# New step orders in three stages of a four-layer kernel, and the soft-MoE normalising products moved from GpSimd to VectorE

## The chip, the cores and the metric

One NeuronCore of a Trainium2 chip runs the whole program. The metric is device microseconds for one launch, lower is better. The kernel before takes 1416.57 us (median of three runs, 1414.6 to 1417.07). The profiled execution took 1420.51 us, of which 1418.7 us lie between its first and last instruction.

## The reference, cut to what matters

The input x is 8 batches of 256 tokens by 128 channels. Four layers follow, each added to x:

```python
x = x + L0_ffn(L0_cond(x))   # per-batch LoRA; gated 8-head attention; gated 8-expert GELU MoE
x = x + L1_ffn(L1_cond(x))   # one SiLU expert per batch; top-k routed GELU experts; layernorm
x = x + L2_ffn(L2_cond(x))   # two of eight tanh-GELU skills + a shared one; soft MoE:
#   logits = x @ phi.T + phi_b, as 64 experts x 32 slots
#   D = softmax(logits over slots); C = softmax(logits over experts)
#   X~ = sum over all tokens of all batches D * x;  Y~ = tanh(layernorm(X~)) @ expert_w
#   Y = sum over experts and slots C * Y~
x = x + L3_ffn(L3_cond(x))   # masked per-batch weights; 16-head rope attention; rmsnorm;
                             # SwiGLU shared + top-2 of 8 experts; rmsnorm
```

L1's routing denominator sums over batches, and so does X~. That cuts the program into stages with a full stop between them.

## The kernel before, in words

All activations stay on chip. The stages are A (L0 and the dense expert of L1), B (the routed experts of L1, the skills of L2, D and X~), a short middle part (Y~), and D (C, Y, and all of L3). Between A and B the routing of all batches is worked out on VectorE and masks pass through a DMA.

In each stage every engine runs its own in-order list of steps, written out as text: `ORDER_A`, `ORDER_B` and `ORDER_D` (L109, L149, L196), with one string for each of SP, PE, ACT, DVE and POOL. A word such as `SI0.3` is step SI0 of batch 3. `walk` (L636) splits the string and calls the stage's step function on each word, so the text alone sets the order of instructions on an engine. Semaphore waits inside the steps hold the data dependences, and nothing else ties the engines together. An engine whose next step is not ready stands still, whatever is ready behind it. Several batches are in flight at once, and the lists differ only in how they interleave.

PSUM is 8 banks, nearly all single-buffered. In stage A four banks (`wide`) hold first the spread router weights (PE SPR0, read by ACT RW0 and RW1), then the hidden units of the MoE (PE MH0, MH1, read by ACT GU0, GU1 with Gelu), then the second spread weights (PE SPR1, read by DVE S8M0, S8M1). One bank (`tail`) serves VT, MOE, UG0, UG1, DN and L1G in turn.

The steps of one batch in stage A, in dependence order: COND, LN0, NH0, NT0, AF0, LOG0, the gate chain (GA0, GB0, GX0, GE0, GTR0), SPR0, RW, S8A, QK (PE L805), QKC, SC, MXA, EX (the attention's Exp), PT, PTC, VT (PE L815), AT, S8B, O1 (PE L839), LN1 to SPR1 (the second gate chain, with GX1), MH, GU, S8M, MOE (PE L862), X1, UG0, SI0 (Silu, L1308), HM0 (DVE L1638), UG1, SI1, HM1, DN (PE L879), L1G, LA, LX (Exp), L1.

In stage B a batch has HID, BC, Z, LN, ZN, ZT (L1's routed experts; HID is a Gelu on ACT), six pairs SG0 to SG5 and SU0 to SU5 (the skills; SG is a tanh-Gelu), UC (PE L965), UT (PE L971), and four rounds of LG, MT, SH, with XT and MC (the soft MoE; SH is an Exp on ACT, L1365, and on DVE the sums and products of D, L1770 to L1774). PE's LG of a round waits until ACT's Exp of the round before has read the bank (L987 after L1365).

In stage D, CL0 to CL7 make exp(logits) in `eC` [128, 16, 256] (PE L1067, ACT L1391), CSA and CSB (POOL) and CSUM (DVE, PE) add it up, REC (DVE L1841) takes the reciprocal `rC`, and CN0 to CN3 multiply a quarter of `eC` each by it, a 128 x 1024 product. CN0 and CN1 are on DVE (L1846), CN2 and CN3 on POOL (L2056). Y0 to Y3 (PE L1080) each use one quarter. The rest is L3: S, V, Q, K, RQ, RK, QM, MX0 to MX3, NM, TS0 to TS3 (attention), AV, AVT, SA, SAT, WO, X5T, G3, FF0, FF1 (Silu), SO, RT0, RT1 with RM0, RM1 (DVE L1936), RR, FIN, OUT.

ScalarE works from a loaded function table. Exp, Gelu, tanh-Gelu and Silu stand in different tables here, and the compiler puts an `ACT_TABLE_LOAD` in front of a step whose function is not in the table at hand. Copy, Identity, Square and Tanh need none. The order of ACT's steps so sets how many loads there are.

Of the kernel before, what the change touches and what calls it, by code (L numbers as in the profile page):

```python
# [66 lines left out]
def _constants():  # L67
# [51 lines left out]
    MH0.4 LOG0.6 UG1.3 MH1.4 DN.3 PT.5 GTR1.4 L1G.3 SPR1.4 GTR0.6 VT.5 COND.7 SPR0.6 AT.5 MOE.4 O1.5 QK.6 NT1.5
    UG0.4 SC.6 NT0.7 LOG1.5 MH0.5 LOG0.7 UG1.4 MH1.5 DN.4 PT.6 GTR1.5 L1G.4 SPR1.5 GTR0.7 VT.6 SPR0.7 AT.6 MOE.5  # L120
    O1.6 QK.7 NT1.6 UG0.5 SC.7 LOG1.6 MH0.6 UG1.5 MH1.6 DN.5 PT.7 GTR1.6 L1G.5 SPR1.6 VT.7 AT.7 MOE.6 O1.7 UG0.6
    UG1.6 NT1.7 DN.6 LOG1.7 MH0.7 L1G.6 MH1.7 GTR1.7 SPR1.7 MOE.7 UG0.7 UG1.7 DN.7 L1G.7""",
    "ACT": """
# [14 lines left out]
    GB1.3 GA0.5 GE1.3 HM1.2 GB0.5 GE0.5 LA.2 S8M0.3 L1.2 S8M1.3 S8B0.4 S8A0.5 S8B1.4 S8A1.5 X1.3 LN0.6 LN1.4
    NH0.6 NH1.4 MXA.5 HM0.3 GA1.4 GB1.4 GA0.6 GE1.4 HM1.3 GB0.6 GE0.6 LA.3 S8M0.4 L1.3 S8M1.4 S8B0.5 S8A0.6
    S8B1.5 S8A1.6 X1.4 LN0.7 LN1.5 NH0.7 NH1.5 MXA.6 HM0.4 GA1.5 GB1.5 GA0.7 GE1.5 HM1.4 GB0.7 GE0.7 LA.4 S8M0.5  # L140
    L1.4 S8M1.5 S8B0.6 S8A0.7 S8B1.6 S8A1.7 X1.5 LN1.6 NH1.6 MXA.7 HM0.5 GA1.6 GB1.6 HM1.5 GE1.6 LA.5 S8M0.6
    L1.5 S8M1.6 S8B0.7 S8B1.7 X1.6 LN1.7 HM0.6 NH1.7 HM1.6 GA1.7 GB1.7 LA.6 GE1.7 L1.6 S8M0.7 S8M1.7 X1.7 HM0.7
# [10 lines left out]
    HID0.0 BC0.0 HID1.0 BC1.0 Z.0 ZT.0 HID0.1 BC0.1 SG0.0 HID1.1 SU0.0 SG1.0 BC1.1 SU1.0 SG2.0 Z.1 SU2.0 SG3.0  # L153
    SU3.0 SG4.0 ZT.1 SU4.0 SG5.0 SU5.0 UC.0 LG0.0 SG0.1 UT.0 HID0.2 SG1.1 SU0.1 MT0.0 HID1.2 SH0.0 SU1.1 SG2.1
    BC0.2 LG1.0 SU2.1 SG3.1 SG4.1 MT1.0 SU3.1 SH1.0 SG5.1 SU4.1 LG2.0 BC1.2 XT0.0 MT2.0 SU5.1 SH2.0 XT1.0 LG3.0
    UC.1 MT3.0 Z.2 SH3.0 MC.0 UT.1 LG0.1 XT2.0 MT0.1 XT3.0 SH0.1 ZT.2 HID0.3 LG1.1 HID1.3 BC0.3 MT1.1 SG0.2
    SH1.1 SU0.2 SG1.2 LG2.1 SU1.2 SG2.2 XT0.1 SG3.2 MT2.1 BC1.3 SU2.2 SG4.2 SH2.1 SU3.2 SG5.2 LG3.1 SU4.2 XT1.1
    Z.3 MT3.1 SU5.2 SH3.1 MC.1 UC.2 XT2.1 LG0.2 XT3.1 ZT.3 UT.2 HID0.4 BC0.4 MT0.2 SG0.3 SH0.2 SU0.3 SG1.3 LG1.2
    SU1.3 SG2.3 HID1.4 BC1.4 SG3.3 MT1.2 SU2.3 SH1.2 SG4.3 SU3.3 LG2.2 SG5.3 XT0.2 Z.4 MT2.2 SU4.3 SH2.2 XT1.2
    LG3.2 SU5.3 ZT.4 MT3.2 UC.3 SH3.2 MC.2 SG0.4 UT.3 LG0.3 SU0.4 XT2.2 SG1.4 HID0.5 MT0.3 XT3.2 SH0.3 SU1.4  # L160
    SG2.4 LG1.3 SU2.4 SG3.4 HID1.5 BC0.5 SG4.4 MT1.3 SU3.4 SH1.3 SG5.4 SU4.4 LG2.3 BC1.5 XT0.3 MT2.3 SU5.4 SH2.3
    XT1.3 LG3.3 UC.4 MT3.3 Z.5 SH3.3 MC.3 UT.4 LG0.4 XT2.3 MT0.4 XT3.3 SH0.4 ZT.5 HID0.6 LG1.4 HID1.6 BC0.6
    MT1.4 SG0.5 SH1.4 SU0.5 SG1.5 LG2.4 SU1.5 SG2.5 XT0.4 SG3.5 MT2.4 BC1.6 SU2.5 SG4.5 SH2.4 SU3.5 SG5.5 LG3.4
    SU4.5 XT1.4 Z.6 MT3.4 SU5.5 SH3.4 MC.4 UC.5 XT2.4 LG0.5 XT3.4 ZT.6 UT.5 HID0.7 BC0.7 MT0.5 SG0.6 SH0.5 SU0.6
    SG1.6 LG1.5 SU1.6 SG2.6 HID1.7 BC1.7 SG3.6 MT1.5 SU2.6 SH1.5 SG4.6 SU3.6 LG2.5 SG5.6 XT0.5 Z.7 MT2.5 SU4.6
    SH2.5 XT1.5 LG3.5 SU5.6 ZT.7 MT3.5 UC.6 SH3.5 MC.5 SG0.7 UT.6 LG0.6 SU0.7 XT2.5 SG1.7 MT0.6 XT3.5 SH0.6
    SU1.7 SG2.7 LG1.6 SU2.7 SG3.7 SG4.7 MT1.6 SU3.7 SH1.6 SG5.7 SU4.7 LG2.6 XT0.6 MT2.6 SU5.7 SH2.6 XT1.6 LG3.6
# [6 lines left out]
    ZT.3 UT.2 HID0.4 MT0.2 SG0.3 SH0.2 SG1.3 SG2.3 HID1.4 SG3.3 MT1.2 SH1.2 SG4.3 SG5.3 MT2.2 SH2.2 ZT.4 MT3.2
    UC.3 SH3.2 MC.2 SG0.4 UT.3 SG1.4 HID0.5 MT0.3 SH0.3 SG2.4 SG3.4 HID1.5 SG4.4 MT1.3 SH1.3 SG5.4 MT2.3 SH2.3
    UC.4 MT3.3 SH3.3 MC.3 UT.4 MT0.4 SH0.4 ZT.5 HID0.6 HID1.6 MT1.4 SG0.5 SH1.4 SG1.5 SG2.5 SG3.5 MT2.4 SG4.5
    SH2.4 SG5.5 MT3.4 SH3.4 MC.4 UC.5 ZT.6 UT.5 HID0.7 MT0.5 SG0.6 SH0.5 SG1.6 SG2.6 HID1.7 SG3.6 MT1.5 SH1.5
    SG4.6 SG5.6 MT2.5 SH2.5 ZT.7 MT3.5 UC.6 SH3.5 MC.5 SG0.7 UT.6 SG1.7 MT0.6 SH0.6 SG2.7 SG3.7 SG4.7 MT1.6
# [1967 lines left out]
```

## Time and profile before

| what | us |
|---|---|
| median of three runs | 1416.57 |
| profiled execution | 1420.51 |
| its span | 1418.7 |
| PE matmul busy | 1128.4 (80%) |
| DVE busy | 764.0 (54%) |
| ACT busy | 497.6 (35%) |
| POOL busy | 213.2 (15%) |
| stage A, COND.0 to the last step | 24 to 380 |
| stage B | 442 to 877 |
| stage D | 900 to 1418.7 |

Busy time is the union of an engine's instructions. PE is the matmul queue and PEld the weight loads beside it. "Idle before" in brackets is the time in which an engine stood still, with the instruction that released it. PEclk is the granted TensorE clock, 1.0 being full speed.

### The profile page before, as it was taken

The numbers are of one execution on the slowest core, as the hardware profiler recorded it, in microseconds if no ns is written. First come the engines' busy times: TensorE is split into PE (matmuls) and PEld (weight loads), VectorE is DVE, ScalarE is ACT, GpSimd is POOL, SyncE is SP. The second block draws the span as 40 slices with busy tenths as digits, with TensorE's granted clock in tenths as the row PEclk, the third lists the DMA queues.
The fourth block names the chain that finished last, engine by engine and source line by source line (L and its number), as shares of the span: only waits on it lengthen the run. The fifth ranks groups of instructions, "written<-read, shape, count | busy, mean of one in ns | idle before, by whom it ended". The sixth has DMA issues, their size and how long they took to land.

```text
span 1418.7 us, 17725 instructions
## 1 busy us (share of the span) xinstructions
PE 1128.4 (80%) x6726; PEld 802.2 (57%) x6726; DVE 764.0 (54%) x1667; ACT 497.6 (35%) x740; POOL 213.2 (15%) x176
## 2 busy tenths in 40 slices
...
DMA packets 13035, 34.96 MB, mean 25 GB/s; under 512 B 3680, under 2 KB 7440, under 8 KB 12179
## 3 DMA queue, kind: packets, MB, share of 16 engines
...
q0 software_dynamic: 32, 0.01, 0.0%
...
## 4 chain that ended last, share of the span: by engine, by line
PE 39%; issue 32%; DVE 12%; ACT 7%; POOLq 4%; DVEq 2%; POOL 1%; ACTq 0%; DMA 0%
PE ps L1080 4%; PE ps L805 4%; PE ps L1213 3%; PE ps L1067 3%; PE ps L815 3%; PE ps L1140 2%; PE ps L862 2%; PE ps L839 2%; PE ps L1156 2%; PE ps L1013 1%; PE ps L1120 1%; DVE arena L1865 1%; POOLq L2025 1%; ACT L1264 1%; ACT L1281 1%
## 5 line engine op out<-in xcount | busy, mean ns | idle before, releaser
L1418 ACT ACTIVATE arena<-ps 128x2048 f32<-128x2048 f32 x32 | 60.1, 1879 | 106.4 <-PE ps L1144 106.4
L1865 DVE TENSOR_REDUCE arena<-ps 128x8 f32<-128x2048 f32 x32 | 73.2, 2287 | 28.1 <-PE ps L1120 28.1
L1013 PE MATMUL ps<-arena 128*128 128x128 f32 x512 | 74.4, 306 | 12.5 <-DVE xacc L1783 6.5
L987 PE MATMUL ps<-arena,uR 128*128 128x512 f32 x128 | 73.7, 659 | 12.6 <-ACT arena L1365 12.2
L1013 PEld LDWEIGHTS ps<-arena 128*128 128x128 f32 x512 | 69.7, 217 | 19.9 <-issue 11.4
L1067 PE MATMUL ps<-uR,arena 128*128 128x256 f32 x256 | 74.0, 387 | 1.4 <-DVE arena L1820 1.4
L1080 PE MATMUL ps<-arena 128*128 128x256 f32 x256 | 64.6, 403 | 10.7 <-DVE arena L1846 10.7
L1213 PE MATMUL ps<-arena 128*128 128x512 f32 x128 | 66.2, 665 | 3.1 <-DVE xacc L1936 2.0
L1391 ACT ACTIVATE arena<-ps 128x512 f32<-128x512 f32 x64 | 38.3, 599 | 78.1 <-PE ps L1068 78.1
L1080 PEld LDWEIGHTS ps<-arena 128*128 128x128 f32 x256 | 50.0, 201 | 26.5 <-DVE arena L1846 12.7
L1770 DVE TENSOR_REDUCE arena<-arena 128x32 f32<-128x1024 f32 x32 | 39.0, 1219 | 48.0 <-ACT arena L1365 48.0
L958 PE MATMUL ps<-x2R,arena 128*128 128x256 f32 x192 | 54.6, 408 | 4.5 <-DVE arena L1751 4.5
L805 PE MATMUL ps<-arena 128*128 128x256 f32 x256 | 58.1, 385 | 0.0
L950 PE MATMUL ps<-x2R,arena 128*128 128x256 f32 x192 | 53.2, 401 | 5.4 <-DVE x2R L1743 3.1
L2056 POOL TENSOR_TENSOR arena<-arena,y1C 128x1024 f32<-128x1024 f32 x16 | 43.1, 2713 | 93.4 <-DVE y1C L1841 93.4
L805 PEld LDWEIGHTS ps<-arena 128*128 128x128 f32 x256 | 48.8, 193 | 7.0
L1140 PE MATMUL ps<-arena,x1C 32*128 32x256 f32 x512 | 44.3, 433 | 9.8 <-ACT arena L1418 7.3
L1760 DVE TENSOR_REDUCE arena<-ps 128x32 f32<-128x1024 f32 x32 | 39.2, 1225 | 22.9 <-PE ps L988 20.8
L965 PE MATMUL ps<-arena 128*128 128x256 f32 x192 | 47.1, 404 | 4.1 <-DVE arena L1751 3.9
L1346 ACT ACTIVATE arena<-ps 128x512 f32<-128x512 f32 x48 | 28.7, 598 | 59.2 <-PE ps L950 59.0
L1067 PEld LDWEIGHTS ps<-uR,arena 128*128 128x128 f32 x256 | 38.8, 190 | 18.8 <-issue 4.0
L1774 DVE TENSOR_TENSOR arena<-arena 128x1024 f32<-128x1024 f32 x32 | 47.2, 1474 | 2.4
...
## 6 DMA issues: line engine op xcount, KB each, us to landing
...
```

The lines of the kernel that those rows point to most:

```text
L805: last = mm(mid[:, j * T:(j + 1) * T], w0[w][:, e, :], S8a[u][:, e, :], start=e == 0, stop=e == E - 1)
L950: last = mm(low[:, 2, j * T:(j + 1) * T], w[:, 2 * h + j, :], x2R[:, b, :], start=True, stop=True)
L958: last = mm(low[:, 3, j * T:(j + 1) * T], w[:, 4 + 2 * h + j, :], x2R[:, b, :], start=True, stop=True)
L987: mm(o, uR[:, b, k * P:(k + 1) * P], phiC[:, col:col + 512], start=True, stop=False)
L1013: last = mm(high[:, 2, t * P:(t + 1) * P], eD[h][:, k, col:col + P], uT[u][:, k, :], start=k == 0, stop=k == 1)
L1067: mm(o, phiC[:, st_ * P:(st_ + 1) * P], uR[:, b, :], start=True, stop=False)
L1080: last = mm(low[:, 1, 0:T], ytl[:, t, :], eC[u][:, t, :], start=t == 0, stop=t == ST - 1)
L1140: mm(scores[:, c, h * T:(h + 1) * T], kR[u][row, t * P:(t + 1) * P], qm[u][row, g, :], start=True, stop=False)
L1213: last = mm(low[:, 2 + c, :], pm[:, 2 + j, k * P:(k + 1) * P], w2e[:, j, c * 512:(c + 1) * 512], start=j == 0, stop=j == 1)
L1418: av(pexp[:, t, gp].rearrange("p c h t -> p (c h t)"), scores[:, :, :].rearrange("p c t -> p (c t)"), ACT.Exp, scale=SCALE3).then_inc(s.sc ...
L1774: V.tensor_tensor(ev, ev, dsum.unsqueeze(2).to_broadcast([P, 32, PSLOT]), ALU.mult).then_inc(s.D_ready, 1)
L1865: V.tensor_reduce(nm[:, k, :, 2 * gp:2 * gp + 2], scores[:, :, :].rearrange("p c (h t) -> p c h t", h=2), X, ALU.max, negate=True).then_in ...
```

## The change

The change has two parts. The first rewrites the order texts of stages A, B and D. Each list holds the same words as before except CN2 and CN3. The interleaving of batches is another one. Lines of stage A's ACT and PE lists around batches 2 to 4, and of the middle and end of stage B:

```diff
 ORDER_A, ACT
-    GU1.1 DN.0 GTR1.1 GX0.3 PTC.2 GTR0.3 LX.0 VC.2 RW0.3 RW1.3 QKC.3 AF1.2 SI0.1 AF0.4 EX.3 GU0.2 GX1.2 SI1.1
-    GU1.2 DN.1 GTR1.2 GX0.4 PTC.3 GTR0.4 LX.1 VC.3 RW0.4 RW1.4 QKC.4 AF1.3 SI0.2 AF0.5 EX.4 GU0.3 GX1.3 SI1.2
+    GX0.4 VC.3 PTC.3 GX1.2 GU0.2 GU1.2 GTR0.4 GTR1.2 AF1.3 RW0.4 SI0.2 RW1.4 AF0.5 SI1.2 GX1.3 GU0.3 DN.2 GX0.5
+    QKC.4 GTR1.3 LX.2 GU1.3 EX.4 VC.4 PTC.4 GTR0.5 RW0.5 SI0.3 RW1.5 SI1.3 QKC.5 DN.3 AF1.4 AF0.6 LX.3 EX.5
+    GX1.4 VC.5 PTC.5 GU0.4 GU1.4 GTR1.4 GX0.6 GTR0.6 AF1.5 SI0.4 RW0.6 RW1.6 SI1.4 GU0.5 GX1.5 GU1.5 QKC.6 DN.4
 ORDER_A, PE
-    SPR1.2 GTR0.4 VT.3 COND.5 SPR0.4 AT.3 MOE.2 O1.3 QK.4 NT1.3 UG0.2 SC.4 NT0.5 LOG1.3 MH0.3 LOG0.5 UG1.2 MH1.3
-    DN.2 PT.4 GTR1.3 L1G.2 SPR1.3 GTR0.5 VT.4 COND.6 SPR0.5 AT.4 MOE.3 O1.4 QK.5 NT1.4 UG0.3 SC.5 NT0.6 LOG1.4
+    L1G.2 GTR1.3 MH1.3 SC.4 VT.4 SPR1.3 PT.4 GTR0.5 AT.4 COND.6 MOE.3 SPR0.5 UG0.3 O1.4 UG1.3 QK.5 DN.3 NT1.4
+    SC.5 L1G.3 NT0.6 LOG1.4 VT.5 PT.5 MH0.4 AT.5 MH1.4 LOG0.6 GTR1.4 SPR1.4 O1.5 MOE.4 GTR0.6 NT1.5 UG0.4 COND.7
+    SPR0.6 LOG1.5 UG1.4 MH0.5 MH1.5 QK.6 DN.4 GTR1.5 SC.6 L1G.4 SPR1.5 NT0.7 VT.6 PT.6 LOG0.7 MOE.5 AT.6 GTR0.7
 ORDER_B, PE
-    UC.3 SH3.2 MC.2 SG0.4 UT.3 LG0.3 SU0.4 XT2.2 SG1.4 HID0.5 MT0.3 XT3.2 SH0.3 SU1.4
-    LG3.7 MT3.7 SH3.7 MC.7 XT2.7 XT3.7""",
+    SG0.5 HID0.6 LG2.3 SU0.5 XT0.3 HID1.6 MT2.3 SG1.5 XT1.3 SH2.3 SU1.5 SG2.5 BC0.6 SU2.5 LG3.3 SG3.5 BC1.6
+    SG4.5 MT3.3 SG5.5 SH3.3 Z.6 SU3.5 LG0.4 XT2.3 SU4.5 MC.3 MT0.4 SU5.5 SH0.4 XT3.3 LG1.4 UC.5 MT1.4 ZT.6 UT.5
+    SH3.5 SU3.7 MC.5 SU4.7 LG0.6 XT2.5 MT0.6 SU5.7 SH0.6 XT3.5 LG1.6 UC.7 MT1.6 UT.7 SH1.6 LG2.6 XT0.6 MT2.6
```

Just before UC.7 the old PE list of stage B has `SH2.6 XT1.6 LG3.6`, the new one `SH0.6 XT3.5 LG1.6`. In stage D the new lists are nearly the old ones. Each batch's TS1 to TS3, RT1 and Y0 to Y3 are interleaved differently on PE, FIN comes ahead of X3 on DVE, and FF1.0 comes next to FF0.0 on ACT, no longer after TS0.1.

The second part moves CN2 and CN3:

```diff
 ORDER_D, DVE  (and the like for every batch; CN2, CN3 leave the POOL list)
-    CSUM.0 REC.0 CN0.0 CN1.0 X3.0 RQ.0
+    CSUM.0 REC.0 CN0.0 CN1.0 CN2.0 CN3.0 X3.0 RQ.0
 step_d, PE
-                    if q < 2:
-                        pe.wait_ge(s.C_ready, at(b, 3, 1 + q))
-                    else:
-                        pe.wait_ge(s.Cp_ready, at(b, 2, q - 2))
+                    pe.wait_ge(s.C_ready, at(b, 4, q))
 step_d, DVE
-                    if b > 0:
-                        dve.wait_ge(s.Cp_ready, at(b - 1, 2, 1))
-                    V.reciprocal(rC, low[:, 0, 0:T]).then_inc(s.C_ready, 1)
-                if n in ("CN0", "CN1"):
+                    V.reciprocal(rC, low[:, 0, 0:T])
+                if n in ("CN0", "CN1", "CN2", "CN3"):
-                    dr()
+                    if q == 0:
+                        dr()
 step_d, POOL
-                if n in ("CN2", "CN3"):
-                    pool.wait_ge(s.C_ready, at(b, 3, 0))
-                    G.tensor_tensor(some, some, rC..., ALU.mult).then_inc(s.Cp_ready, 1)
```

## Rows read from the trace of the kernel before

**Rows 1.** Windows by stage (stretch, its us): PE, PEld, DVE, ACT, POOL busy, clock, DMA share, GB/s.

```profile
22.00:380.00 358.00, 294.44 (x1752) 254.33 (x1752) 158.51 (x650) 152.26 (x235) 25.85 (x48) 0.91 0.05 18
442.00:877.00 435.00, 375.80 (x1672) 244.75 (x1671) 268.38 (x392) 165.69 (x229) 39.57 (x29) 0.94 0.06 22
925.00:1418.70 493.70, 416.07 (x3050) 273.30 (x3048) 264.52 (x410) 161.02 (x250) 97.25 (x68) 0.91 0.01 3
```

**Rows 2.** Windows in stage A: two whole batch periods, and two short stretches.

```profile
173.68:215.74 42.06, 35.52 (x221) 31.42 (x220) 19.46 (x80) 19.84 (x30) 3.23 (x6) 0.92 0.04 10
215.74:258.99 43.25, 37.91 (x222) 33.18 (x221) 19.52 (x80) 19.80 (x30) 3.23 (x6) 0.84 0.04 10
196.00:204.00 8.00, 3.17 (x14) 2.44 (x14) 2.88 (x22) 7.88 (x12) 0.69 (x1) 0.98 0.00 1
204.00:216.00 12.00, 10.29 (x66) 9.23 (x65) 5.87 (x31) 4.62 (x10) 0.00 (x0) 0.73 0.12 34
```

**Rows 3.** Timeline of PE in stage A: VT.1, QK.2, VT.5, O1.7.

```profile
73.04 3.74 PE L815 MATMUL ps<-arena 128*128 128x128 f32 x32
100.84 7.10 PE L805 MATMUL ps<-arena 128*128 128x256 f32 x32
252.63 6.51 PE L815 MATMUL ps<-arena 128*128 128x128 f32 x32 [0.21 <-DVE arena L1649]
344.68 3.74 PE L839 MATMUL ps<-arena 128*128 128x128 f32 x32
```

**Rows 4.** Chain of waits in stage A, 192 to 206 us: start, us, what.

```profile
192.27 1.28 ACT L1308
...
201.20 1.28 ACT L1308
...
203.54 1.96 PE ps L879 x4
```

**Rows 5.** Table loads by line, first and last of eleven groups: xcount | busy, mean ns.

```profile
L1346 ACT ACT_TABLE_LOAD x26 | 33.4, 1283 | 0.5
...
L1232 ACT ACT_TABLE_LOAD x1 | 1.3, 1283 | 1.6 <-PEq L2140 1.6
```

**Rows 6.** Stage B: timeline of PE at UT.1 and UT.7.

```profile
515.70 0.39 PE L971 MATMUL ps<-cst,uR 128*128 128x128 f32 x2
...
823.14 0.44 PE L971 MATMUL ps<-cst,uR 128*128 128x128 f32 x2 [0.42 <-ACT uR L1350]
```

**Rows 7.** Window of three batch periods of stage B.

```profile
569.51:726.44 156.93, 139.64 (x642) 91.92 (x642) 102.40 (x151) 67.07 (x91) 16.25 (x12) 0.97 0.09 31
```

**Rows 8.** Chain of waits in stage B's last part: the Exp of three rounds.

```profile
842.51 1.03 ACT arena L1365
...
855.81 1.03 ACT arena L1365
...
863.97 1.03 ACT arena L1365
```

**Rows 9.** The products by source line: ns min/median/max, first and last start.

```profile
L1846 DVE TENSOR_TENSOR arena<-arena,y1C x16: 1227/3137/3405, 917.4 to 1304.8; 128x1024 f32<-128x1024 f32 x16
L2056 POOL TENSOR_TENSOR arena<-arena,y1C x16: 2337/2350/3328, 917.4 to 1303.6; 128x1024 f32<-128x1024 f32 x16
L1774 DVE TENSOR_TENSOR arena<-arena x32: 1225/1226/3017, 483.7 to 866.7; 128x1024 f32<-128x1024 f32 x32
```

**Rows 10.** Stage D: Y.0 on PE, CN.5 on DVE, the loads of FF1.0 and TS1.1.

```profile
920.87 8.75 PE L1080 MATMUL ps<-arena 128*128 128x256 f32 x32 [5.35 <-DVE arena L1846]
1188.76 6.42 DVE L1846 TENSOR_TENSOR arena<-arena,y1C 128x1024 f32<-128x1024 f32 x2
1011.52 1.28 ACT L1442 ACT_TABLE_LOAD   x1
1013.43 1.28 ACT L1418 ACT_TABLE_LOAD   x1
```

**Rows 11.** Window of one batch period of stage D.

```profile
1180.39:1236.31 55.92, 50.59 (x388) 33.83 (x388) 35.59 (x53) 20.41 (x32) 13.66 (x9) 0.97 0.01 3
```

More of the change, by code:

```diff
@@ L118 @@
-    DN.2 PT.4 GTR1.3 L1G.2 SPR1.3 GTR0.5 VT.4 COND.6 SPR0.5 AT.4 MOE.3 O1.4 QK.5 NT1.4 UG0.3 SC.5 NT0.6 LOG1.4
[L119 to L122, printed above, removed]
@@ L129 @@
-    GU1.4 DN.3 GTR1.4 GX0.6 PTC.5 GTR0.6 LX.3 VC.5 RW0.6 RW1.6 QKC.6 AF1.5 SI0.4 AF0.7 EX.6 GU0.5 GX1.5 SI1.4
-    GU1.5 DN.4 GTR1.5 GX0.7 PTC.6 GTR0.7 LX.4 VC.6 RW0.7 RW1.7 QKC.7 AF1.6 SI0.5 EX.7 GU0.6 SI1.5 GX1.6 GU1.6
-    DN.5 GTR1.6 PTC.7 LX.5 VC.7 SI0.6 SI1.6 AF1.7 DN.6 GU0.7 GX1.7 LX.6 GU1.7 GTR1.7 SI0.7 SI1.7 DN.7 LX.7""",
+    QK.1 NT1.0 NT0.2 VT.1 SC.1 LOG1.0 MH0.0 PT.1 MH1.0 LOG0.2 AT.1 GTR1.0 SPR1.0 O1.1 MOE.0 GTR0.2 NT1.1 UG0.0
+    COND.3 SPR0.2 LOG1.1 UG1.0 MH0.1 MH1.1 QK.2 DN.0 GTR1.1 SC.2 L1G.0 SPR1.1 NT0.3 VT.2 PT.2 LOG0.3 MOE.1 AT.2
@@ new lines @@
+    GTR0.3 UG0.1 COND.4 SPR0.3 O1.2 UG1.1 NT0.4 QK.3 DN.1 NT1.2 SC.3 L1G.1 LOG0.4 LOG1.2 VT.3 PT.3 MH0.2 AT.3
+    MH1.2 GTR1.2 GTR0.4 COND.5 SPR1.2 O1.3 MOE.2 NT1.3 SPR0.4 UG0.2 LOG1.3 NT0.5 UG1.2 MH0.3 LOG0.5 DN.2 QK.4
+    L1G.2 GTR1.3 MH1.3 SC.4 VT.4 SPR1.3 PT.4 GTR0.5 AT.4 COND.6 MOE.3 SPR0.5 UG0.3 O1.4 UG1.3 QK.5 DN.3 NT1.4
+    SC.5 L1G.3 NT0.6 LOG1.4 VT.5 PT.5 MH0.4 AT.5 MH1.4 LOG0.6 GTR1.4 SPR1.4 O1.5 MOE.4 GTR0.6 NT1.5 UG0.4 COND.7
+    SPR0.6 LOG1.5 UG1.4 MH0.5 MH1.5 QK.6 DN.4 GTR1.5 SC.6 L1G.4 SPR1.5 NT0.7 VT.6 PT.6 LOG0.7 MOE.5 AT.6 GTR0.7
@@ new lines @@
+    UG0.5 SPR0.7 O1.6 UG1.5 QK.7 DN.5 NT1.6 SC.7 L1G.5 LOG1.6 VT.7 PT.7 MH0.6 AT.7 MH1.6 GTR1.6 SPR1.6 O1.7
+    MOE.6 NT1.7 UG0.6 LOG1.7 MH0.7 UG1.6 MH1.7 GTR1.7 SPR1.7 DN.6 L1G.6 MOE.7 UG0.7 UG1.7 DN.7 L1G.7""",
+    "ACT": """
+    AF0.0 GX0.0 GTR0.0 RW0.0 RW1.0 AF0.1 QKC.0 EX.0 GX0.1 VC.0 PTC.0 GTR0.1 RW0.1 RW1.1 QKC.1 AF1.0 AF0.2 VC.1
+    EX.1 GU0.0 PTC.1 GX1.0 GU1.0 GTR1.0 GX0.2 GTR0.2 AF1.1 SI0.0 RW0.2 RW1.2 SI1.0 GU0.1 GX1.1 GU1.1 QKC.2 DN.0
+    GTR1.1 EX.2 LX.0 AF0.3 VC.2 PTC.2 GX0.3 GTR0.3 SI0.1 RW0.3 RW1.3 SI1.1 AF0.4 QKC.3 DN.1 AF1.2 EX.3 LX.1
@@ new lines @@
+    GX0.4 VC.3 PTC.3 GX1.2 GU0.2 GU1.2 GTR0.4 GTR1.2 AF1.3 RW0.4 SI0.2 RW1.4 AF0.5 SI1.2 GX1.3 GU0.3 DN.2 GX0.5
+    QKC.4 GTR1.3 LX.2 GU1.3 EX.4 VC.4 PTC.4 GTR0.5 RW0.5 SI0.3 RW1.5 SI1.3 QKC.5 DN.3 AF1.4 AF0.6 LX.3 EX.5
+    GX1.4 VC.5 PTC.5 GU0.4 GU1.4 GTR1.4 GX0.6 GTR0.6 AF1.5 SI0.4 RW0.6 RW1.6 SI1.4 GU0.5 GX1.5 GU1.5 QKC.6 DN.4
+    GTR1.5 EX.6 AF0.7 LX.4 VC.6 PTC.6 GX0.7 GTR0.7 SI0.5 RW0.7 RW1.7 SI1.5 QKC.7 DN.5 AF1.6 EX.7 LX.5 GX1.6 VC.7
+    PTC.7 GU0.6 GU1.6 GTR1.6 AF1.7 SI0.6 GU0.7 GX1.7 GU1.7 SI1.6 GTR1.7 DN.6 LX.6 SI0.7 SI1.7 DN.7 LX.7""",
@@ L138 @@
[L138 to L142, printed above, removed]
@@ L152 @@
     "PE": """
[L153 to L167, printed above, removed]
@@ L174 @@
[L174 to L178, printed above, removed]
```

141 lines of the change are left out of this document (77 added, 64 removed).

## The prediction, made before the changed kernel ran

> **What bounds the kernel now.** I read the page first, then the windows by stage, then the chain of waits and the timelines of the stretches where PE stands still. PE is busy 80% of the span, and no other engine above 54%, so each stage is worth what PE's idle time in it is worth. By stage [rows 1] PE is idle 358.0 - 294.4 = 63.6 us in A, 435.0 - 375.8 = 59.2 in B, and 493.7 - 416.1 = 77.6 in D.
>
> In A the idle time has one clear cause. A batch period takes 42.06 or 43.25 us, with PE busy 35.52 and 37.91 [rows 2]. From 196 to 204 us ACT is busy 7.88 of 8.00 us and PE 3.17 [rows 2]. The chain of waits there is ACT's queue. Between 192.27 and 201.20 us it makes five table loads (Silu, Exp, Gelu, Exp, Silu), each 1.28 us, and the second Silu lets HM1 and then DN start at 203.54 [rows 4]. So two Silu steps of one batch, with nothing of their own between them but UG1, stand five loads apart. PE pays a second time. In the 12 us behind this gap its granted clock is 0.73 [rows 2], a mix of 1.2 and 2.4 GHz. The same VT takes 6.51 us there and 3.74 where PE had been busy before it [rows 3].
>
> In B three periods take 156.93 us, of which PE is busy 139.64 [rows 7]: 52.3 and 46.5 a batch, clock 0.97. In D a period takes 55.92, PE busy 50.59, clock 0.97 [rows 11]. The rest of D's idle time is in its first two batches and its last two, where nothing is there to fill in.
>
> **Table loads, counted.** The order text fixes them. If I walk the old ACT lists and count a load at each step whose function (Exp, Gelu, tanh-Gelu, Silu) differs from the last one, I get 51 in A, 59 in B and 17 in D, and with the one at the start 128. The trace has 128, in eleven groups from x26 to x1, mean 1283 ns [rows 5]. So the count can be trusted for the new text, which gives 38, 50 and 15: 24 fewer, 24 x 1.283 = 30.8 us of ACT's time. That alone is no gain in the end. It is one only where ACT's queue ends a wait.
>
> The Trainium skill (ScalarE: Activation LUTs, What ACT_TABLE_LOAD costs) puts a switch at 2.66 us, the load and a drain of 1.38. The row disagrees: from the load at 201.20 to DN at 203.54 [rows 4] are 2.34 us, which hold the load, the Silu and HM1. By the page the loads left out would be 24 x 2.66 = 64 us of ACT's time, by the rows 30.8.
>
> **Stage A.** Its new order puts SI0 and SI1 of a batch next to each other (one Silu load, where there were two in most batches), GU0 and GU1 often too, and gives PE the steps of another batch in the meantime. I walked the new lists by hand over four batches with durations of the trace, asking at each PE step for its latest input. From QK.5 on, for example: PE has QK until 7.1, and ACT's QKC ends at 7.7, while PE does DN.3 and NT1.4. EX.5 ends at 14.1, behind LX.3 and one load, while PE is at VT.5 until 14.8. GU0.4 and GU1.4 end at 18.2 and 20.5, while PE has MH0.4, AT.5, MH1.4 and LOG0.6 until 20.3. Only SPR1.4 waits, 0.6 us. In the four batches I find PE waits of 0.2 to 1.9 us a batch where it is now about 6, and none in front of DN.
>
> PE's own work of a period at full clock is its busy time by the clock: 35.52 x 0.92 = 32.7, 37.91 x 0.84 = 31.8 [rows 2], and since the clock is a mean over idle time too I take 33. With the waits I found it would be 34.5. I take 36, because a hand walk leaves out small delays, and PE will not stay at full clock throughout. The stretch in which this counts goes from QK.2 (100.84) to the end of O1.7 (344.68 + 3.74 = 348.42), 247.6 us [rows 3]. In the new order QK.2 starts some 5 us later, since MOE.0, UG0.0, UG1.0 and MH.1 now stand ahead of it. Five periods of 36 to QK.7 make 180, and from there to the end of O1.7 are QK, VT, O1, two MH and small steps, 28 us. The end of O1.7 so comes at 5 + 180 + 28 = 213 after the old start of QK.2, which is 35 us earlier. What follows (the second gate chain of batch 7, MOE.7, UG to L1G) is the same latency chain, MOE.6 now included in it. I take **-34**. The bounds are -17 (13 loads x 1.283 and nothing else) and -47 (34.5 a period, and half a load more on each of the chain's first batches), and below both, a loss, the third rival.
>
> **Stage B.** Before, UT.1 to UT.7 take 823.14 - 515.70 = 307.4 us [rows 6]. The new order repeats each batch, with 6 loads in a period for 7.7. I walked that period: PE work 46.5 [rows 7], and waits of 0.5, 0.5, 0.65, 0.65 and 0.3 us (SG0 on X2, SG4 and SG5 on the Gelu before them, SU5 on SU4's product, UT on UC's copy), together 49. Of the six intervals the first has two LG rounds of four and the last no L1 part: 40 + 4 x 49 + 42.5 = 278.5, 29 us less. But this order carries its soft-MoE rounds half a batch behind. The old list has all four rounds of batch 6 issued before UC.7, the new one two. So two more rounds stand in the last part, where each round is a bare chain of LG, MT, SH, Exp and DVE. Two such rounds took 863.97 - 842.51 = 21.5 us [rows 8]. Net 21.5 - 29 = **-8**. If the period is 52.3 as now, stage B loses: -9 to -13 for the shorter intervals against 21.5, about +10. If it is 47.3, it gains 15.
>
> **Stage D.** The products: DVE's take 1.23 us at their shortest and 3.14 at the median, POOL's 2.35 [rows 9]. Stage B's L1774, of the same shape, has a median of 1.23 and a maximum of 3.02 [rows 9]. So two engines at once make each other slow, and a pair on DVE takes 6.42 us [rows 10]. Four alone on DVE take 4 x 1.23 = 4.9, 1.5 us less than the two now, and POOL loses 16 instructions. If all four stayed at 3.14 it would be 12.6, 6.1 us more a batch. I take 1.23, since POOL has only the two-column RS2 in that stretch. What this gives the end: Y.0 waited 5.35 us for the first product [rows 10] and would now wait 3.2, 2 us. Batch 1 gives 1.6 likewise. In the steady batches RM0 comes behind the products and RT1 behind RM0, but PE has TS1 and Y0 in between, so I count 0.4 each for five batches. FF1.0 beside FF0.0 saves two loads on the chain (the rows at 1011.52 and 1013.43), 2.6 us [rows 10]. That makes 8.2, of which I take **-7**. Hidden and counted as nothing: POOL's QM, CSA and CSB, which become free earlier but start on DVE's rope and ACT's exponentials; REC's wait for POOL, long over when REC comes; FIN ahead of X3 (PE's last products of Y and TS3 cover it; without that cover S of the next batch is 0.6 us later).
>
> **Sum.** 34 + 8 + 7 = 49. 1418.7 - 49 = 1369.7 of span, 1371.5 for the profiled execution, which had 1.8 around its span. That execution was 3.9 us above the median, so 1416.6 - 49 = 1367.6, or **1368 us**. The forecast's own range is 1355 to 1383.
>
> **Rivals.**
> - *More than that.* A keeps the hand walk's 34.5, B its 47.3, and the clock stays up: 47 + 15 + 10 = 72, so 1345 us. For it: behind a busy stretch VT is always 3.74. Against: every period of this trace, even of B and D, has 5 us of small waits. Chance 0.12.
> - *Only the loads go.* The in-order queues find new places to stand: A gains 13 x 1.283 = 16.7, B 0, D 7, together 24, so 1393. For it: B and D have one load fewer and still small waits all over. Against: the half-clock stretches of A are bound to its one long gap. Chance 0.18.
> - *The order leaves the end where it is* and only the products count, -5, 1412. It would need ACT's queue in A not to be what PE waits for, and the chain says it is. Chance 0.03.
> - *The wide banks become the loop, slower.* In A they are held from SPR0 to the end of S8M1 of the same batch. The new list bunches four MH and four GU of two batches around the second gate chain (GX1, GE1, GTR1). If that hold is longer than the 42.65 us of today's period [rows 2], it sets the period. At 47 us it costs 4.35 x 6 = 26, against 15 gained in B and D, so 1416.6 + 11 = 1428. It turns the sign from 45.2 us on. For it: one late GX1 behind a Gelu load holds everything. Against: in my walk MH0.4 to S8M1.4 is some 10 us. Chance 0.07.
>
> The forecast has 0.60. Faster by over 0.2% (2.8 us, about what a measurement of this kernel can tell) is 0.60 + 0.12 + 0.18 and most of the 0.03, 0.91. Within that 0.02, slower 0.07. The range 1346 to 1402 takes in the first two rivals and leaves out the last two.
>
> **What would show it.** Right, in the changed trace: 104 table loads; windows between starts of QK that average under 38 us, with a clock above 0.93, and VT at 3.7; no wait of DN on HM1 above 1 us; stage A shorter by 25 to 40 us. In B a period near 49, and a last part (UT.7 to the end) some 20 us longer than now. The products at 1.23 us, 32 on DVE. Wrong: new waits of PE in A behind L1264 or L1281, a clock in A as now, a period of B at 52, or products of 2 us and more.

## The result and the profile after

The changed kernel took 1329.8 us (median of 4 runs, 1320.4 to 1337.3) against 1415.7 of the kernel before: ratio 0.939, 95% interval 0.933 to 0.945. Six more runs on another chip gave 1334.3 us (1323.2 to 1337.2), ratio 0.940 (0.937 to 0.943). The gain is some 85 us, 6%. I had forecast 1368 with a range down to 1346, so the direction was right and the size much too small. The profiled execution took 1331.6 us with a span of 1329.8.

First the windows of the changed kernel: the three stages, then QK.2 to QK.7 in A, three periods of B, one of D (stretch, its us, busy time of PE, PEld, DVE, ACT and POOL, granted clock, DMA share, GB/s).

```profile
22.00:338.50 316.50, 278.92 (x1752) 242.53 (x1752) 160.47 (x650) 135.22 (x222) 28.62 (x48) 0.95 0.06 20
401.50:801.40 399.90, 357.44 (x1658) 231.59 (x1656) 260.21 (x390) 150.01 (x215) 39.32 (x28) 0.97 0.07 24
838.59:1329.80 491.21, 415.80 (x3062) 271.53 (x3062) 270.34 (x429) 159.96 (x248) 59.84 (x54) 0.92 0.01 3
108.87:273.27 164.40, 159.08 (x1066) 141.35 (x1065) 94.96 (x375) 79.09 (x133) 15.53 (x25) 0.98 0.05 13
539.90:679.84 139.94, 134.06 (x643) 88.17 (x642) 97.75 (x151) 58.01 (x84) 17.86 (x13) 1.00 0.10 35
1094.41:1150.30 55.89, 50.97 (x388) 33.44 (x388) 34.56 (x55) 20.75 (x32) 8.02 (x7) 0.97 0.01 3
```

A is 316.5 us where it was 358.0 [rows 1], B's three periods are 139.9 where they were 156.9 [rows 7], and this one period of D is as it was [rows 11]. To see what the five intervals of A had lost before, here is the same stretch (QK.2 to QK.7) of the kernel before, its window and PE's waits (engine, line, released by: us in total, times, longest), and then PE's waits in the changed kernel.

```profile
100.84:310.41 209.57, 181.77 (x1092) 159.44 (x1091) 95.68 (x393) 97.81 (x149) 15.23 (x28) 0.89 0.04 10
```

```profile
PE ps L879 <- DVE arena L1638: 19.3, 4, 4.8
PE ps L783 <- DVE arena L1604: 5.3, 5, 2.2
PE ps L815 <- DVE arena L1649: 1.5, 5, 0.5
```

```profile
PE ps L814 <- DVE arena L1645: 1.8, 3, 0.8
PE ps L768 <- DVE nT L1560: 1.1, 1, 1.1
PE ps L761 <- ACT arena L1265: 1.0, 1, 1.0
```

Idle time fell from 27.8 to 5.3 us. DN's wait (L879, 19.3 us) is gone and nothing has taken its place. But PE's *busy* time fell too, by 22.7 us. Some 5 us of that is work that now stands ahead of QK.2: the new text has MH0, MH1 and LOG1 only four times between QK.2 and QK.7, the old one five times (26 matmuls fewer; MH0 and MH1 take 19.3 us for 80 matmuls and 15.4 for 65 in the runs without loads). The other 18 or so are the clock, 0.89 then and 0.98 now. PE's timeline in the changed kernel, at the QK of batches 2, 3, 4 and 6, VT.5, QK.7 and O1.7 (start, us, shapes, wait before it):

```profile
108.87 7.10 PE L804 MATMUL ps<-arena 128*128 128x256 f32 x32
...
136.85 7.10 PE L804 MATMUL ps<-arena 128*128 128x256 f32 x32
...
177.95 7.09 PE L804 MATMUL ps<-arena 128*128 128x256 f32 x32
...
216.52 5.43 PE L814 MATMUL ps<-arena 128*128 128x128 f32 x32 [0.84 <-DVE arena L1645]
...
245.95 7.10 PE L804 MATMUL ps<-arena 128*128 128x256 f32 x32
...
273.27 7.10 PE L804 MATMUL ps<-arena 128*128 128x256 f32 x32
...
296.70 3.84 PE L838 MATMUL ps<-arena 128*128 128x128 f32 x32
```

VT.5 had 6.51 us [rows 3] and has 5.43. The other seven take 3.73 to 3.81, or 5.44 in two cases; before, every VT from VT.2 on took 4.89 to 6.52. The five intervals average 32.9 us, but they are not alike: the new list takes two batches at a time, with 28.0 us from QK.2 to QK.3, 41.1 to QK.4, then 27.5, 40.5 and 27.3. The stretch holds three short intervals and two long ones. A period, taken over two batches, is 34.5 us (QK.2 to QK.4) and 34.0 (QK.4 to QK.6).

The table loads (ACT's groups by line, first and last of eleven: count | busy, mean ns) add up to the 104 that I had counted:

```profile
L1342 ACT ACT_TABLE_LOAD x23 | 29.5, 1283 | 0.4
...
L1228 ACT ACT_TABLE_LOAD x1 | 1.3, 1283 | 1.6 <-PEq L2130 1.6
```

In D, the products by source line (ns min/median/max) and PE at Y.0 and Y.1:

```profile
L1841 DVE TENSOR_TENSOR arena<-arena,y1C x32: 1218/1221/1228, 841.7 to 1216.7; 128x1024 f32<-128x1024 f32 x32
```

```profile
842.96 9.75 PE L1076 MATMUL ps<-arena 128*128 128x256 f32 x32 [3.15 <-DVE arena L1841]
880.42 3.78 PE L1076 MATMUL ps<-arena 128*128 128x256 f32 x8 [3.71 <-DVE arena L1841]
```

All 32 products take 1.22 us, and Y.0 waits 3.15 us, as forecast (3.2; before 5.35 [rows 10]). Its matmuls take 9.75 us, though, where they took 8.75 [rows 10], so of the 2.2 us that the wait lost only 1.2 arrive at the next CSUM.

The stages of all profiled executions, cut at the start of PE's last L1G of A, of its first and last UC of B, and of its first CSUM of D. The columns are us: A until L1G.7; routing and B's start; UC.0 to UC.7; B's last part and the expert stage; D; the span.

```
                      A  to UC.0  UC.0-7  to CSUM.0      D     span
before            376.8     85.7   354.7       97.1  504.4   1418.7
changed           334.8     82.1   305.3      116.5  491.2   1329.8
changed, again    330.9     85.7   306.9      117.6  491.2   1332.4
A's lists alone   329.2     85.8   354.5       97.1  504.5   1371.1
B's lists alone   375.9     85.7   306.9      117.6  501.2   1387.2
part D alone      376.5     85.8   354.5       97.2  491.3   1405.2
products alone    374.7     85.7   354.7       97.1  495.0   1407.2
before, no loads  319.4     84.1   338.6       95.5  498.0   1335.6
changed, no loads 327.3     81.7   307.8      116.9  491.2   1325.0
before, Silu out  351.5     85.4   354.7       95.3  504.7   1391.6
changed, +15 loads 340.3    85.6   305.2      118.7  491.3   1341.1
XT moved          330.2     81.7   305.3      110.5  483.5   1311.1
XT moved, filled  329.1     85.7   306.8       99.4  482.4   1303.4
filled only       334.5     80.1   306.2      110.2  490.0   1321.0
```

One thing can be read off at once: the two profiles of the changed kernel differ by 4 us in A and by -4 in the column behind it, so a difference under 4 us in either column alone says nothing of a change. Their sum, the time until UC.0, is 416.9 and 416.6, and is the safer figure.

### The profile page after: what moved, and what is told of

It reads as the page before. It is cut to its first block, busy times and chain, and to the rows that moved or that the text cites. A ratio compares the mean times of both kernels' runs of the same rounds, so it can differ in the third digit from the quotient of the medians.

```text
span 1329.8 us, 17686 instructions
## 1 busy us (share of the span) xinstructions
PE 1094.6 (82%) x6726; PEld 775.4 (58%) x6726; DVE 751.5 (57%) x1683; ACT 468.3 (35%) x716; POOL 174.2 (13%) x160
## 4 chain that ended last, share of the span: by engine, by line
PE 63%; DVE 13%; issue 12%; ACT 4%; DVEq 3%; POOLq 2%; POOL 1%; DMA 0%; ACTq 0%
PE ps L1076 5%; PE ps L804 4%; PE ps L986 4%; PE ps L1012 4%; PE ps L1209 4%; PE ps L949 3%; PE ps L957 3%; PE ps L964 3%; PE ps L1066 2%; PE ps L814 2%; PE ps L1136 2%; DVE arena L1860 2%; PE ps L838 2%; PE ps L861 2%; PE ps L1152 2%
## 5 line engine op out<-in xcount | busy, mean ns | idle before, releaser
L1012 PE MATMUL ps<-arena 128*128 128x128 f32 x512 | 67.5, 287 | 9.8 <-DVE xacc L1779 5.7
L1012 PEld LDWEIGHTS ps<-arena 128*128 128x128 f32 x512 | 63.7, 200 | 15.8 <-issue 8.3
L1076 PEld LDWEIGHTS ps<-arena 128*128 128x128 f32 x256 | 50.6, 203 | 22.3 <-DVE arena L1841 8.8
L804 PEld LDWEIGHTS ps<-arena 128*128 128x128 f32 x256 | 50.2, 197 | 7.7
L1931 DVE TENSOR_TENSOR xacc<-ps,arena 128x1024 f32<-128x1024 f32 x16 | 19.6, 1224 | 53.2 <-PE ps L1209 53.2
L1209 PEld LDWEIGHTS ps<-arena 128*128 128x128 f32 x128 | 25.4, 208 | 35.6 <-issue 29.2
```

The costliest lines, as they stand in the source:

```text
L804: last = mm(mid[:, j * T:(j + 1) * T], w0[w][:, e, :], S8a[u][:, e, :], start=e == 0, stop=e == E - 1)
L1012: last = mm(high[:, 2, t * P:(t + 1) * P], eD[h][:, k, col:col + P], uT[u][:, k, :], start=k == 0, stop=k == 1)
L1076: last = mm(low[:, 1, 0:T], ytl[:, t, :], eC[u][:, t, :], start=t == 0, stop=t == ST - 1)
L1209: last = mm(low[:, 2 + c, :], pm[:, 2 + j, k * P:(k + 1) * P], w2e[:, j, c * 512:(c + 1) * 512], start=j == 0, stop=j == 1)
```

## Experiments

**The parts one by one.** Each stage's lists alone, the rest as before:

```diff
 ORDER_A = {            # a_order: only this dictionary is the new one
-    ...                # b_order: only ORDER_B
+    ...                # d_part: only ORDER_D, and the products' code
```

> The kernel before with the new lists of stage A alone. Theory 1 (the stages are separate, and A's gain is where the two traces show it): A ends 41.6 us earlier, the routing part behind it gives back or adds up to 4 us, B and D take what they took before; 1416 - 42 to 46, so 1370 to 1374, with PE periods of A near 33 and stage A's clock near 0.95. Theory 2 (part of the gain is a shared lift, a clock or a queue that only all stages together change): A gives clearly less than 40 when alone, 1385 or more.

Measured: 1374.4 us (1372.9 to 1376.4), ratio 0.972 (0.970 to 0.973), -41. Theory 1 holds, and the stages behind A took what they took before. PE's clock from QK.2 to QK.7 is 0.99.

> The kernel before with the new lists of stage B alone. Theory 1: B's seven UC intervals go from 354.7 to 305, its last part from 59.9 to 79 us, net -30, so 1386. My prediction's size for B (periods of 49 for three engines' small waits) would give -8, 1408. Theory 2 (B gains because A leaves its data and queues earlier): between -8 and -20.

Measured: 1388.8 us (1385.6 to 1389.1), ratio 0.981 (0.979 to 0.982), -27. Theory 1 is nearest. UC.0 to UC.7 gives -47.8, the part behind it +20.5. B does this with A as it was, so it does not live on A's earlier end.

> The kernel before with all of part D: the new lists of stage D and the four products on DVE. Theory 1: -13 us, 1403, most of it in the first three CSUM intervals (1.2, 5.4 and 4.2 us) and 0 to 2 in the later ones. By the prediction -7, 1409.

Measured: 1406.5 us (1404.8 to 1407.0), ratio 0.994 (0.992 to 0.995), -9, between my two forecasts. Its profile has D shorter by 13, with the intervals that theory 1 gives; the medians have 9.

```diff
 ORDER_D DVE   ... REC.1 MX3.0 CN0.1 NM.0 CN1.1
+              CN2.1 CN3.1                       # likewise for every batch, with the code of the products
 ORDER_D POOL  CSA.1 CSB.1
-              CN2.1 CN3.1
```

> The kernel before with its old lists in A, B and D, only CN2 and CN3 of each batch taken from GpSimd's list and put behind CN1 on VectorE. Theory 1 (products at 1.23 us when alone; what they give is Y's wait in the first batches only): -3 to -5 us, 1411 to 1413, each product 1.23 us. Rival (the products are hidden and the gain of D is its order and its two loads fewer): within 1 us of 1416. Second rival (all of D's gain): -10 or more.

Measured: 1409.1 us (1408.3 to 1411.2), ratio 0.996 (0.995 to 0.997), -6, a little more than theory 1. So two thirds of D's gain are the products, and what the new lists add is 2.6 us, as forecast. That this is FF1.0 beside FF0.0 is not shown. CSUM.1 to CSUM.2 goes from 56.4 to 54.2, and with the new lists to 51.0, but both loads of rows 10 stand behind CSUM.2 (1006.11), and the new PE list also puts CSUM.2 ahead of NM.1. CSUM.2 to CSUM.3, where the loads stood, goes from 60.8 to 58.1 and to 56.6, and a later interval loses 2.5 again.

The three parts add to -76, and the ratios multiply to 0.9465, where the whole has 0.940 (0.937 to 0.943). So the whole gains some 9 us more than the sum. The stage times of the profiles show no such thing: A's lists (415.0 until UC.0), B's (424.5 from there until CSUM.0) and part D (491.3) add up to 1330.8, and the changed kernel has 1329.8. The same code of D took 501.2 to 504.7 us in the profiles with its old lists, so stages of profiles add up only within a few us. Where the 9 us between the medians lie stays open.

> The changed kernel once more, to see what the sum of its parts leaves over. Alone the lists of A gave -40.8 us, those of B -26.5, part D -8.7, together -76.0, which would be 1339; the first four runs had a median of 1329.8, from 1320 to 1337. Theory 1 (the stages are separate and the wide spread is the run's): a median of 1333 to 1340. Theory 2 (together they give more than their sum, through the clock): 1326 to 1331 again.

Measured: 1334.3 us, ratio 0.940 (0.937 to 0.943); the time lies in theory 1's range, but the kernel before was 3 us slower on this chip too, and the ratio is the first one again. So it decides nothing on the 9 us.

**Is it the loads?** Gelu, tanh-Gelu and Silu replaced in all stages:

```diff
-    ... low[:, 2, :], ACT.Gelu_apprx_tanh)
+    ... low[:, 2, :], ACT.Tanh)          # likewise every Gelu and Silu
```

> The kernel before, old lists, with Gelu, tanh-Gelu and Silu replaced by Tanh in all stages, a function that shares Exp's table: this leaves out nearly all of the 128 table loads and changes the activation values. Theory L (loads in ACT's queue are what the old lists suffer from in A): the five-load gap ahead of DN closes, periods of A fall from 42.8 to 36 or less, A gives -35 or more; B falls by 5 to 20, D by 5; together about 1350. Theory O (the old lists put the steps in the wrong places whatever the loads): A gives -10 to -20 only and the whole ends at 1385 or more.

Measured: 1333.4 us (1325.5 to 1337.4), ratio 0.939 (0.935 to 0.942), 17 us faster than theory L's 1350. The old lists with one load are as fast as the new lists with 104. Here are the window of QK.2 to QK.7 and all of PE's waits in it:

```profile
97.68:260.97 163.29, 160.90 (x1091) 141.78 (x1090) 95.12 (x393) 53.04 (x115) 15.25 (x28) 1.00 0.05 13
```

```profile
PE ps L815 <- DVE arena L1649: 2.0, 5, 0.5
PE ps L879 <- DVE arena L1638: 0.3, 1, 0.3
```

The same list that had waited 19.3 us at DN waits 0.3. Its period is 32.7 us and its clock 1.00, with the same work in 20.9 us less of busy time (181.77 and 160.90). In A 51 loads cost 376.8 - 319.4 = 57.4 us, and 59.0 until UC.0.

> The changed kernel with the same replacement of the functions: nearly all of its 104 table loads left out. Theory L: the new lists hide what loads are left, so this gains 5 to 15 us on the changed kernel (in the ramps and tails of the stages, where nothing covers a load) and stands 10 to 25 us from the old lists without loads. Theory O: it stands 50 us or more ahead of the old lists without loads.

Measured: 1326.3 us (1323.2 to 1327.0), ratio 0.935 (0.933 to 0.937). The new lists lose 8 us by their loads in all (1334.3 on the same chip), which is in theory L's 5 to 15, all of it in A (7.7 until UC.0), nothing that can be seen in the middle of B or in D. They stand only 7 us from the old lists without loads, under theory L's 10 to 25. The window of QK.2 to QK.7 without loads:

```profile
107.17:271.35 164.18, 158.95 (x1066) 141.28 (x1065) 94.46 (x375) 51.47 (x110) 15.35 (x25) 0.98 0.05 13
```

With loads ACT is busy 27.6 us more there, and the stretch takes 164.40: in the middle of A the loads cost 0.2 us. What they cost lies at A's two ends, 1.7 us ahead of QK.2 and 5.5 between QK.7 and L1G.7.

Theory L holds for A. In B it holds for a part. UC.0 to UC.7 is 354.7 with the old lists, 338.6 without loads, 305 to 308 with the new ones either way. The order alone gives two thirds of that, but it pays 19 to 21 us back behind UC.7. From UC.0 to CSUM.0 the order alone is worth 9 us (434.1 without loads and 424.7), where with loads it is worth 27 to 30 (451.8, and 421.8 or 424.5). And without loads the new lists of A are slower than the old ones, by 8 us (327.3 and 319.4) or 5.5 until UC.0 (409.0 and 403.5). That is their price. It is there at QK.2 already, which starts 9.5 us later (107.17 and 97.68).

```diff
-    av(h1[u][:, j, :], tail[:, 0:T], ACT.Silu, bias=...)     # stage A, lists of before
+    av(h1[u][:, j, :], tail[:, 0:T], ACT.Tanh, bias=...)
```

> The kernel before, old lists everywhere, with only the two Silu of each batch of stage A replaced by Tanh, which shares Exp's table; that changes the activation values of A's experts. The five loads ahead of DN become two (Gelu, Exp). Theory L, in its narrow form (the loads that split the two Silu steps are what A loses by): periods of A fall from 42.8 to 34-36, A ends 38 us or more earlier, about 1375. Rival (every load in ACT's queue counts alike): A has lost half of its loads, so half of the 58 us that A gained without any load, about -29, 1388.

Measured: 1392.3 us (1388.8 to 1393.5), ratio 0.981 (0.979 to 0.983). A has 32 loads in place of 51 and ends 25.3 us earlier: 1.33 us a load, against 1.13 over all 51. My narrow form (38 us or more) falls, and the rival, that every load counts alike, comes near with its 29. The Silu loads are not the whole of it. In this order a load costs on average about its own length.

```diff
+    if j == 1:
+        av(tiny[:, 0:1], cpart[:, 0:1], ACT.Exp)              # lists of the changed kernel
     act.wait_ge(s.up_mm, at(b, 2, j))
```

> The changed kernel, with one Exp of a single column put between SI0 and SI1 of every batch on ACT in stage A, which adds 16 loads (a load to Exp and one back to Silu), so 54 where the old lists had 51; 2.57 us and a small activation of some 0.2 us a batch. Theory L (a load between the Silu steps stands on PE's way to DN): A loses 10 to 22 us, 1343 to 1356, with waits of PE on the way to DN and a clock in A under 0.93. Rival (new places count, the number of loads does not, ACT has the time): A loses less than 5 us, 1334 to 1339.

Measured: 1342.2 us (1339.2 to 1342.9), ratio 0.946 (0.944 to 0.948), +8 to +12. A has 53 loads now, two more than the old lists had, and still ends at 340.3 where those ended at 376.8. The window of QK.2 to QK.7:

```profile
106.32:274.11 167.79, 160.92 (x1066) 142.60 (x1065) 95.20 (x375) 95.21 (x150) 15.53 (x25) 0.97 0.05 13
```

ACT is 16 us busier than in the changed kernel and the stretch 3.4 us longer. The rest of the loss lies behind QK.7, in A's last two batches, which have no later batch beside them. So both theories miss their numbers. Until UC.0 the old lists take 462.5 us with their loads and 403.5 without, the new ones 416.9 and 409.0: loads cost 59 us in the one order and 8 in the other. So it is not the number of loads. That it is whether PE has other work while a load runs fits the 0.2 us in the middle and the loss at the ends, but no run changed that by itself.

**B's last part.** The 12-us rounds of the changed kernel, ACT's Exps of rounds in turn (SH2.6, SH3.6, SH0.7, SH1.7), and one of PE's XT there:

```profile
739.52 1.02 ACT L1361 ACTIVATE arena<-ps 128x1024 f32<-128x1024 f32 x1 [3.90 <-PE ps L998]
747.69 1.02 ACT L1361 ACTIVATE arena<-ps 128x1024 f32<-128x1024 f32 x1 [1.73 <-PE ps L998]
759.78 1.02 ACT L1361 ACTIVATE arena<-ps 128x1024 f32<-128x1024 f32 x1 [4.00 <-PE ps L998]
767.95 1.03 ACT L1361 ACTIVATE arena<-ps 128x1024 f32<-128x1024 f32 x1 [1.73 <-PE ps L998]
```

```profile
753.34 2.05 PE L1012 MATMUL ps<-arena 128*128 128x128 f32 x16
```

They stand 8.2 and 12.1 us apart in turn. In the long rounds XT0 or XT2, VectorE's addition, XT1 or XT3, all stand ahead of SH on PE.

```diff
 ORDER_B PE
-    LG2.6 XT0.6 MT2.6 XT1.6 SH2.6 LG3.6 MT3.6 SH3.6 MC.6 LG0.7 XT2.6 MT0.7 XT3.6 SH0.7 LG1.7 MT1.7 ...
+    LG2.6 XT0.6 MT2.6 SH2.6 LG3.6 XT1.6 MT3.6 SH3.6 MC.6 LG0.7 XT2.6 MT0.7 SH0.7 LG1.7 XT3.6 MT1.7 ...
```

XT1.7 moves likewise, and so do the additions of these XT in VectorE's list.

> The changed kernel, and in B's last part only XT1 and XT3 of batches 6 and 7 moved: behind LG3 and behind LG1 of the next batch, so that each round of LG, MT, SH and Exp has one XT in its gap behind LG instead of two ahead of SH in every other round. The tail's Exps stand 8.2 and 12.2 us apart in turn now. Theory 1 (a PE list too long ahead of SH makes the 12.2): three such rounds fall to 8.2, -12 us, 1318 to 1325. Rival (VectorE's chain of SH and LG sets it, or the XT in the new place delays MT): rounds of 10 to 12 remain, -3 us or less.

Measured: 1315.4 us (1307.0 to 1325.0), ratio 0.928 (0.925 to 0.932), 19 us under the changed kernel's 1334.3 on the same chip. But the six rounds from SH1.6 on are 7.8, 10.1, 10.1, 9.9, 8.5 and 8.1 us (10.4, 8.2, 12.1, 8.2, 12.2 and 8.2 before), and the column to CSUM.0 falls by 6 to 7 only. Another 8 are in D, with not a line of D changed (see below). Each round of 10 has a row of PE like this one in it:

```profile
747.14 3.78 PE L1012 MATMUL ps<-arena 128*128 128x128 f32 x16
```

XT took 2.05 us in the rounds of the changed kernel's profile.

```diff
+    fill_after = {"MT": 2, "SH": 3}       # in B's last part, behind each of them; XT moved as above
+    ...
+    mm(low[:, 0, :], identb[:, :], cbf[:, 0:512], start=True, stop=True)
```

> The version with XT1 and XT3 moved in B's last part, and in that part two or three 128x512 matmuls of constants into a free bank behind each MT and SH, fourteen behind the last SH, so that PE has no long gap. In the version without them rounds took 7.8, 10.1, 10.1, 9.9, 8.5 and 8.1 us, with XT at 3.78 us in the long ones and 2.05 in the short. Theory C (gaps in PE's work bring the half clock, and that makes the rounds long): XT at 2.05, rounds at 7.8 to 8.2, the last two XT at 2 us: -6 to -10 us against the version without, about 1308. Rival (the clock does not follow these gaps, or the added matmuls delay MT and SH): 0 or slower.

Measured: 1307.4 us (1305.2 to 1316.4), ratio 0.924 (0.921 to 0.926). Every one of the six rounds takes 7.7 to 8.1 us. Theory C holds. Windows from UC.7 to B's last addition, first of the version without the added matmuls, then with them, and two rows of the latter's PE (three added matmuls, then an XT):

```profile
717.11:791.80 74.69, 58.32 (x216) 34.98 (x215) 45.88 (x64) 10.35 (x18) 0.03 (x1) 0.77 0.00 1
```

```profile
721.70:785.20 63.50, 55.22 (x261) 29.39 (x264) 45.53 (x63) 10.47 (x18) 0.00 (x0) 1.00 0.00 1
```

```profile
744.01 0.82 PE L1029 MATMUL ps<-cbf,identb 128*128 128x512 bf16 x3
...
748.27 2.02 PE L1012 MATMUL ps<-arena 128*128 128x128 f32 x16 [0.20 <-DVE arena L1778]
```

The granted clock goes from 0.77 to 1.00, all of it at the level of 2.4 GHz, and 45 matmuls *more* take 3.1 us *less* of PE's busy time.

> The changed kernel with the same added matmuls and its lists as they are. Its rounds are 8.2 and 12.2 us in turn, at mostly full clock, so by theory C only the half-clock parts of LG and the last two XT change: -3 to -5 us, and the 12.2 stays near 12. By the rival: 0 or slower.

Measured: 1328.9 us (1322.8 to 1331.0), ratio 0.938 (0.936 to 0.939), some 4 us under the changed kernel by the ratios. Its rounds are 10.4, 8.2, 11.0, 7.8, 10.4 and 8.1. The column to CSUM.0 is 116.5 or 117.6 in the changed kernel, 110.5 with XT moved, 110.2 with the filler alone, and 99.4 with both. So each edit gives 6 to 7 us by itself, and both together some 4 more than their sum. The old lists, with two rounds less to do in that column, had 97.1. The version with both, 1307 us, is faster than either kernel.

**Why one kernel's runs differ by 1.3%.** D has the same code in "changed" and "XT moved". Here is the period from CSUM.4 to CSUM.5 in both, first in "changed", then in "XT moved":

```profile
1036.70:1094.40 57.70, 52.45 (x388) 34.01 (x388) 34.68 (x55) 20.75 (x32) 8.03 (x7) 0.94 0.01 3
```

```profile
1023.50:1078.50 55.00, 50.86 (x388) 33.73 (x388) 34.52 (x55) 20.72 (x32) 8.01 (x7) 0.97 0.01 3
```

VectorE and ACT are equal to 0.2 us. The clock is 0.94 and 0.97, the period 57.7 and 55.0. PE is busy 1.6 us longer in the first, and it has one wait more, of 1.2 us (L1123, on VectorE); the short waits around CSUM and FF1 are the same in both. The mean clock of a period does not fix its length: periods of 54.7 us have 1.00 in "changed" (CSUM.6 to CSUM.7) and 0.97 in "XT moved" (CSUM.5 to CSUM.6). I read the spread of single runs as this; it was not tested by itself.

## Why the prediction was too small

Two terms of the sum were too small: the -8 of stage B and the -34 of stage A. In the profiles the whole went down by 89 us where the sum had 49. Of the 40 missing, 22 are in B (-30), 12 in A with the routing behind it (-46), 6 in D (-13). By the medians of the parts alone B has -27, A -41, D -9, and 9 us belong to none of them.

- *Table loads, 104*: right, and the price of one as well (1283 ns). What failed is what I let a load cost. I wrote of the 24 loads that go; the runs show that the new order hides most of the other 38 of A too. 51 loads cost the old A 59 us until UC.0 and 38 loads cost the new one 8, so some 50 us were to be had, and 5 are paid back.
- *Stage B, -8; measured -27 alone, -30 in the profile*: the largest miss. The loss of 21.5 us for two more rounds at the end was right (+19.4 and +20.5). The step that failed is "PE work 46.5 ..., together 49" and its use for all four middle intervals. UT.1 to UT.7 was to be 278.5 and is 262.7. 46.5 was the old period's busy time with its half-clock parts in it; times its clock of 0.97 it would have been 45. The period is 46.65, of which PE works 44.7 at clock 1.00 and waits 2.0 (7 us for three periods). The interval behind UT.2 is 42.9, where I had put 49 there too (6 us), the one before it 37.5 for 40, and 4.7 us between UC.0 and UT.1 I had not looked at. By the runs without loads the old list gains 18 us from UC.0 to CSUM.0 when the loads go, and the order adds 9.
- *Stage A, -34; measured -42 and -46 until L1G.7*, and -41 of the time with A's lists alone. The mechanism was right: the wait at DN closes and the clock comes up. The failing step is "Five periods of 36 to QK.7 make 180", measured 164.4, in two ways. "I take 36, because a hand walk leaves out small delays" put 1.5 us a period on a walk that was right: 34.5, measured 34.5 and 34.0 over pairs of batches. The 33 for PE's own work was right as well. The old list's work at clock 1.00 is 32.2 a period, and 35.52 x 0.92 and 37.91 x 0.84 had said 32.7 and 31.8. And the stretch holds no five whole periods, since one batch's MH0, MH1 and LOG1, 5 us, stand ahead of QK.2. The other terms hid part of this miss. QK.2 came 8.0 us later, not 5. The way from QK.7 to the end of O1.7 took 27.3 (28). What follows O1.7 until L1G.7 was taken as the same chain and is 34.2 us where it was 28.4, so 5.9 us of the gain are given back there. That the total is off by 8 to 12 only, and not by 15, is luck. Of the 45 us that the five intervals lost, 22.5 are idle time, some 18 are clock and 5 the work that was moved. The forecast had seen the VT of 6.51 us but not that every period held such stretches.
- *Stage D, -7; measured -9*, products 6 of it (5.6 in the prediction's steps), loads and order 3 (2.6). The sum is right. Row by row it is not shown: the profile with the products alone has D 9.4 us shorter, by 1.2, 2.2, 2.7, 0.3 and 1.0 us in the first five intervals and by -0.2 and 1.7 in the next two, where the forecast had 2, 1.6 and 0.4 for each of five.
- *Rivals.* "More than that" (1345) named the right mechanism, both walks kept and the clock up, with a chance of 0.12; even it is 10 to 15 us short, since its B is 15 and not 27. The range of 1346 to 1402 was said to take in the first two rivals, but the first lies 1 us below it. "Only the loads go" and the wide banks as the loop are excluded: no wait of PE in A's middle is above 1.1 us.
- Of the Trainium skill's price of a switch (ScalarE: Activation LUTs, What ACT_TABLE_LOAD costs), 2.66 us, the runs allow less: with all 127 that can go taken out, the old lists gain 85 us, 0.67 a load. The 51 in the stage where ACT bounds most, A, cost 1.13 each, the 19 that go with the Silu steps 1.33. Nothing in the runs shows the drain of 1.38 us that the page adds: the next instruction starts as soon as the load ends, and the load as soon as the step before it ends, as in these rows of the kernel before.

```profile
198.63 1.02 ACT L1281 ACTIVATE arena<-ps 128x1024 f32<-128x1024 f32 x1
199.67 1.28 ACT L1264 ACT_TABLE_LOAD   x1
200.96 0.22 ACT L1264 ACTIVATE arena<-arena 128x16 f32<-128x16 f32 x1
```
